# Attention and expert kernel: second-pass score units issued in pairs, and both layer norms applied by GpSimd

## The reference

```python
def _layernorm(x, eps=1e-05):
    return (x - mean(x)) / sqrt(var(x) + eps)

def attn(x, W_qkv, b_qkv, W_proj, b_proj):
    qkv = x @ W_qkv.T + b_qkv                       # 3 x 16 heads x 8
    logits = einsum('bthc,bshc->bhts', q, k) * scale
    attn = softmax(where(causal, logits, -inf))
    return einsum('bhts,bshc->bthc', attn, v) @ W_proj.T + b_proj

def ffn(x, Wg, alpha, ln_w, ln_b, fc1_w, fc1_b, fc2_w, fc2_b):
    top_vals, top_idx = top_k(x @ Wg, 2)
    comb = (one_hot(top_idx) * softmax(top_vals)).sum() * alpha
    for e in range(8):
        a = gelu(layernorm(x, ln_w[e], ln_b[e]) @ fc1_w[e] + fc1_b[e])
        out += (a @ fc2_w[e] + fc2_b[e]) * comb[:, e]

x = x + attn(_layernorm(x), ...)
x = x + ffn(_layernorm(x), ...)
```

## Time and profile before

| | |
|---|---|
| median of 3 runs | 556.99 us (554.35 to 557.75) |
| the profiled execution | 553.86 us |
| its span, first to last instruction | 551.8 us |
| mean granted TensorE clock | 0.964 of full |
| busy: TensorE, weight loads | 484.6, 306.0 us |
| busy: VectorE, ScalarE, GpSimd | 350.7, 319.7, 256.5 us |
| span by stage | attention to about 382 us, experts to 528 us, sums and output to 552 us |

### The profile page before, as it was taken

One profiled execution on the slowest core, in us unless ns is written; L12 is line 12 of the kernel. 1 busy time (PEld: TensorE's weight loads), 2 busy tenths in 40 slices (PEclk: granted clock), 3 DMA queues, 4 the chain that ended last, 5 costly groups with the idle time before them and its releaser, 6 DMA issues.

```text
span 551.8 us, 13646 instructions
## 1 busy us (share of the span) xinstructions
PE 484.6 (88%) x4736; PEld 306.0 (55%) x4736; DVE 350.7 (64%) x900; ACT 319.7 (58%) x693; POOL 256.5 (46%) x371
## 2 busy tenths in 40 slices
PE   3278999999899999999999999888999999999920
PEld 1134445445455545545544555444888888888920
DVE  3386857778868968977877887864355722222326
ACT  2126677667667656667666766666555546465610
POOL 5755132243644445454454362352766774445520
PEclk9679999999999999999999999998999999999985
DMA  2514124133225134233314230226884697666539
GB/s 67 131 35 118 43 83 116 64 92 111 94 64 148 54 85 137 72 94 113 96 63 118 72 97 27 77 70 198 248 303 154 212 317 206 212 191 194 157 138 325
DMA packets 54068, 71.67 MB, mean 130 GB/s; under 512 B 11889, under 2 KB 39704, under 8 KB 54000
## 3 DMA queue, kind: packets, MB, share of 16 engines
q1 hardware_dynamic: 48336, 59.48, 36.4%
q0 software_dynamic: 4512, 8.70, 4.8%
q10 hardware_dynamic: 1152, 2.62, 1.4%
HBM read 36.49 MB, written 20.94 MB: 104 GB/s over the span
## 4 chain that ended last, share of the span: by engine, by line
PE 64%; DVE 24%; DMA 4%; issue 3%; POOL 2%; ACT 1%; SPq 1%; POOLq 0%; DVEq 0%; ACTq 0%
DVE row_max L976 11%; PE scores L783 11%; PE acc_bank L720 11%; PE acc_bank L792 10%; PE banks L702 7%; PE banks L706 6%; PE scores L682 4%; PE scores L687 4%; PE banks L651 3%; DMA y_in<-y_dram 2%; PE banks L638 2%; DVE xn L931 2%; PE banks L735 2%; PE banks L800 1%; PE banks L747 1%
## 5 line engine op out<-in xcount | busy, mean ns | idle before, releaser
L976 DVE TENSOR_REDUCE row_max<-scores 128x2 f32<-128x1024 f32 (+2 forms) x192 | 197.3, 1041 | 67.4 <-PE scores L687 63.0
L849 ACT ACTIVATE probs<-banks 128x512 f32<-128x512 f32 (+2 forms) x384 | 183.1, 531 | 89.9 <-PE banks L706 89.3
L706 PE MATMUL banks<-stack_q,stack_k 64*128 64x256 bf16 (+3 forms) x512 | 107.3, 296 | 0.0
L702 PE MATMUL banks<-causal_back,select 64*128 64x128 bf16 (+1 forms) x768 | 100.4, 237 | 5.6 <-DVE max_rows L982 3.1
L879 ACT ACTIVATE hidden<-scores,w_in 128x256 f32<-128x256 f32 (+1 forms) x156 | 62.9, 455 | 61.2 <-PE scores L783 61.0
L720 PE MATMUL acc_bank<-probs,v 128*32 128x512 f32 (+3 forms) x1024 | 95.3, 445 | 0.5 <-issue 0.4
L1321 POOL DMA_INDIRECT y_dram<-y,z_in x71 | 69.7, 982 | 53.0 <-DVE y L1160 36.2
L1282 POOL DMA_INDIRECT z_dram<-z,pos x64 | 62.9, 983 | 45.4 <-DVE pos L1068 27.3
L682 PE MATMUL scores<-causal,select 64*128 64x128 bf16 (+1 forms) x768 | 70.4, 241 | 14.6 <-DMA stack_k<-parts 8.2
L687 PE MATMUL scores<-stack_k,stack_q 64*128 64x256 bf16 (+3 forms) x512 | 75.4, 302 | 0.0
L702 PEld LDWEIGHTS banks<-causal_back,select 64*128 64x128 bf16 x768 | 49.1, 94 | 45.3 <-ACT probs L849 18.9
(11 more groups left out here) (172 smaller groups left out, 508.2 us busy)
## 6 DMA issues: line engine op xcount, KB each, us to landing
w_in<-in_wpack SPq DMA_DIRECT2D x39, 516.0 KB, 3.9
o_dram<-oT SPq DMA_DIRECT2D x32, 256.0 KB, 2.4
stack_k<-parts SPq DMA_DIRECT2D x47, 128.0 KB, 2.4
stack_q<-parts SPq DMA_DIRECT2D x45, 128.0 KB
z_in<-z_dram SPq DMA_DIRECT2D x32, 132.0 KB, 3.8
xt<-in_x SPq DMA_DIRECT2D x8, 256.0 KB, 3.4
onT<-o_dram SPq DMA_DIRECT2D x8, 256.0 KB, 3.4
o_inv<-inv_dram SPq DMA_DIRECT2D x8, 256.0 KB, 3.5
```

The lines of the kernel that those rows point to most:

```text
L702: pe.matmul(cols[:, :, 0:P], select[rows(t), step, :], causal_back[rows(t), step, 0:len(heads), :], start=step == 0, stop=False, skip_grou ...
L706: mm = pe.matmul(cols[:, i, :], k[rows(t), at_head, blk * P:blk * P + P], q[rows(t), at_head, blk * P:T], start=False, stop=True, skip_gro ...
L849: act.activation(probs_of(n), columns(n), ACT.Exp, scale=SCALE).then_inc(s_exp, 1)
L976: dve.tensor_reduce(largest, used, AX.X, ALU.max).then_inc(s_max, 1)
```

## The change

It has three parts. First, `pass2` is issued for two units at once: it waits for both banks, writes the masks of both alternately, then the scores of both alternately, and raises `s_pass2` once for the pair. The pair stands at odd ticks, `LAG` goes from 26 to 27, and with it the product with v moves to even ticks and the copy of the output by one tick. Second, `xn` and `z` are computed by GpSimd instead of VectorE, in four tensor_scalars each, at the same places of the schedule; z still waits for the earlier dispatches from its buffer. Third, the second norm gets its own `mean_var_two`, and VectorE waits before it overwrites the moments until GpSimd has used them.

```diff
-LAG = 26
+LAG = 27
...
-        if 0 <= n - LAG < G * UNITS:
-            add(("pass2", n - LAG))
+        if 0 <= n - LAG < G * UNITS and (n - LAG) % HALVES == 0:
+            add(*(("pass2", n - LAG + t) for t in range(HALVES)))
...
             def pass2(n):
-                g, u, w, heads = unit_of(n)
+                if n % HALVES > 0:
+                    return
+                g, u, w, _ = unit_of(n)
                 b, hg = divmod(g, NG)
-                wait_bank(pe, ("pass2", n))
+                for t in range(HALVES):
+                    wait_bank(pe, ("pass2", n + t))
                 if u == 0:
                     pe.wait_ge(s_mrow[g % 2], 16 * (g // 2 + 1))
-                cols = columns(n)
+                cols = [columns(n + t) for t in range(HALVES)]
+                heads = [UNIT[u + t][1] for t in range(HALVES)]
                 blk = NT - w // P
                 q, k = stack[0][b % STACKS], stack[1][b % STACKS]
-                t = place(g, heads[0])[0]
                 for step in range(2):
-                    pe.matmul(cols[:, :, 0:P], select[rows(t), step, :], causal_back[rows(t), step, 0:len(heads), :],
-                              start=step == 0, stop=False, skip_group_check=True)
-                for i, h in enumerate(heads):
-                    at_head = place(g, h)[1]
-                    mm = pe.matmul(cols[:, i, :], k[rows(t), at_head, blk * P:blk * P + P], q[rows(t), at_head, blk * P:T],
-                                   start=False, stop=True, skip_group_check=True)
+                    for t in range(HALVES):
+                        pe.matmul(cols[t][:, :, 0:P], select[rows(t), step, :], causal_back[rows(t), step, 0:len(heads[t]), :],
+                                  start=step == 0, stop=False, skip_group_check=True)
+                for i in range(len(heads[0])):
+                    for t in range(HALVES):
+                        at_head = place(g, heads[t][i])[1]
+                        mm = pe.matmul(cols[t][:, i, :], k[rows(t), at_head, blk * P:blk * P + P], q[rows(t), at_head, blk * P:T],
+                                       start=False, stop=True, skip_group_check=True)
                 mm.then_inc(s_pass2, 1)
...
             def pass2(n):
                 g, u, w, _ = unit_of(n)
-                wait(act, s_pass2, n + 1)
+                wait(act, s_pass2, n // HALVES + 1)
...
             def aggregate(*_):
-                mean_variance()
+                wait(dve, s_xn, variance_no[0])
+                mean_variance(mean_var)
...
-            def make_z(b):
+            def find_ratio(b):
                 wait(dve, s_rtwo, b + 1)
-                wait(dve, s_disp[b % 2], 16 * 2 * NT * (b // 2))
-                normalise(z[:, b % 2, 0, :, 0:C], xt[:, NT * b:NT * b + NT, :], rstd_two[:, 0, :]).then_inc(s_z, 1)
                 dve.tensor_tensor(ratio[:, :], var_two[:, 0, :], rstd_two[:, 0, :], ALU.mult).then_inc(s_ratio, 1)
...
+            def normalise(dst, src, moments, by):
+                return pool.tensor_scalar(dst, src, moments[:, 0:1], by, ALU.subtract, ALU.mult)
+
+            def ln_apply(b, n):
+                if n == 0 and b > 0:
+                    wait_filled(pool, ("xnT", b - 1))
+                wait(pool, s_rstd, b + 1)
+                ins = normalise(xn[:, n, :], xt[:, NT * b + n, :], mean_var[:, n, :], rstd[:, n:n + 1])
+                if n == NT - 1:
+                    ins.then_inc(s_xn, 1)
+
+            def make_z(b):
+                wait(pool, s_rtwo, b + 1)
+                wait(pool, s_disp[b % 2], 16 * 2 * NT * (b // 2))
+                for n in range(NT):
+                    last = normalise(z[:, b % 2, 0, n, 0:C], xt[:, NT * b + n, :], mean_var_two[:, n, :], rstd_two[:, 0, n:n + 1])
+                last.then_inc(s_z, 1)
```

More of the change, by code:

```diff
@@ L279, in build @@
         mean_var = sb("mean_var", [P, NT, 2])
+        mean_var_two = sb("mean_var_two", [P, NT, 2])
         var_eps = sb("var_eps", [P, NT])
@@ L530, in stack_up @@
                 else:
-                    sp.wait_ge(s_pass2, (b - STACKS + 1) * NG * UNITS)
+                    sp.wait_ge(s_pass2, (b - STACKS + 1) * NG * UNITS // HALVES)
                 if b >= STACKS and i == 0 and part == 0:
@@ L602, in load_tile @@
                     sp.wait_ge(s_pass1, G * SCORED)
-                    sp.wait_ge(s_pass2, (B - 1) * NG * UNITS)
+                    sp.wait_ge(s_pass2, (B - 1) * NG * UNITS // HALVES)
                 sp.wait_ge(s_table, list_of(i) + 1)
@@ L910, in variance, with mean_variance @@
                 stats_no[0] += 1
-            def mean_variance():
+            def mean_variance(dst):
                 dve.wait_ge(s_stats, stats_no[0])
                 for n in range(NT):
-                    last = dve.bn_aggr(mean_var[:, n, :], stats[:, n, :])
+                    last = dve.bn_aggr(dst[:, n, :], stats[:, n, :])
                 link(last)
             def aggregate(*_):
-                mean_variance()
+                wait(dve, s_xn, variance_no[0])
+                mean_variance(mean_var)
                 dve.tensor_scalar(var_eps[:, :], mean_var[:, :, 1], EPS, None, ALU.add).then_inc(s_var, 1)
@@ L923, in aggregate_two @@
             def aggregate_two(b):
[L925 to L931, removed]
-                                             ALU.subtract, ALU.mult)
-                return last
+                wait(dve, s_z, b)
+                mean_variance(mean_var_two)
+                dve.tensor_scalar(var_two[:, 0, :], mean_var_two[:, :, 1], 1.0 + EPS, EPS * EPS, ALU.mult, ALU.add)
+                dve.tensor_scalar(var_two[:, 1, :], mean_var_two[:, :, 1], EPS, None, ALU.add).then_inc(s_two, 1)
             def init_stacks():
@@ L940, in ln_stats @@
                 variance(xt[:, NT * b:NT * b + NT, :])
-            def ln_apply(b, n):
-                if n == 0 and b > 0:
-                    wait_filled(dve, ("xnT", b - 1))
-                wait(dve, s_rstd, variance_no[0])
-                ins = normalise(xn, xt[:, NT * b:NT * b + NT, :], rstd, (n,))
-                if n == NT - 1:
-                    ins.then_inc(s_xn, 1)
             def split(b, i, step):
@@ L1052, in combine @@
                 link(dve.tensor_reduce(alpha_of[:, :, :].rearrange("p j n -> p (j n)"), by_alpha[:, :, :], AX.X, ALU.add))
+                wait(dve, s_disp[b % 2], 16 * 2 * NT * (b // 2))
                 dve.tensor_copy(z[:, b % 2, :, :, ID].bitcast(I32), token_ids[:, :, NT * b:NT * b + NT])
@@ L1327, in _ @@
             walk({"init_masks": init_masks, "init_stacks": init_stacks, "init_second": init_second, "init_third": init_third, "init_v": init_v, "init_experts": init_experts,
-                  "init_blank": init_blank, "init_wide": init_wide, "dispatch": dispatch, "turn_y": turn_y, "ln_agg": rsqrt, "r_root": rsqrt_two, "split": split, "max_parts": split_max,
+                  "init_blank": init_blank, "init_wide": init_wide, "dispatch": dispatch, "turn_y": turn_y, "ln_agg": rsqrt, "ln_apply": ln_apply, "r_root": rsqrt_two, "r_z": make_z, "split": split, "max_parts": split_max,
                   "residual": residual, "r_exp": second_gate})
```

4 lines of the change are left out of this document (2 added, 2 removed).

## The result

The changed kernel takes 602.72 us (median of 4 runs, 601.86 to 606.04) against 555.76 us (554.35 to 557.75) for the kernel before on the same chip: ratio 1.087, 95% interval 1.084 to 1.090. That is 47 us slower, 27 us above the upper end of the forecast range.

A forecast was written before the change was run, and what follows sets the result against it. TensorE, busy 484.6 of 551.8 us, was taken as the bound. Savings and waits net -0.4 us a batch, -2.8 over seven; with +2.6, +0.4 and +1.4 that is +1.6: 555.5, or 558 us on the median's footing, range 540 to 576.

The forecast's parts named there:

- The savings: Pass 2 on TensorE: in 17 of 24 pairs a batch the second unit's own time goes, 6.4 us a batch.
- (a) to (d): Waits added in attention because a pair needs both banks free and written: 1.7, 1.8, 1.0 and 0.6 us a batch.
- the credit: 0.5 us a batch off the added waits, since VectorE's max_rows already held pair 3's second unit in some groups.
- (a): Two-block to one-block pair, once a group: waiting for ScalarE cancels the four one-block savings, 1.7 us a batch.
- (b): Pair 2 waits for both banks of pair 1, the maximum's transpose holding the third: 0.45 us a group, 1.8 a batch.
- (e): xn on GpSimd behind a dispatch DMA: its transpose 1.0 us later, 0.4 of savings lost, 1.4 us a batch.
- (f): z in a steady batch on GpSimd: ready about 0.5 us ahead of its transpose, so no cost.
- (g): z of the last batch, in the expert stage, queued behind a scatter on GpSimd: 2.6 us later, once.
- (h): GpSimd's queue at the start: xn of batch 0 0.3 us later, of batch 1 0.4 earlier, counted as nothing.
- (i): LAG 27 at the end: one more pass 2 step without pass 1, 0.4 us, and bare bank waits, 1.4 us.
- Slow GpSimd: Rival: GpSimd's tensor_scalar takes 0.9 us, making xn and z late, 4 us a batch, 586 us; chance 0.12.
- the clock: Rival: longer idle at xn's transposes and late z lowers TensorE's granted clock, 14 us in all, 572 us; chance 0.17.

The follow-up runs named there:

- e17: Kernel before with only pass 2 in pairs and LAG 27, norms on VectorE, on a chip where before takes 554 us: ratio 1.0067.
- e1: Kernel before with only pass 2 in pairs and LAG 27, norms on VectorE, first measurement, on a slower chip: ratio 0.9999.
- e13: Kernel before with only pass 2 in pairs and LAG 27, norms on VectorE, repeated on a slower chip: ratio 0.997.
- e8: Changed kernel with xn normalised for only 40 of 128 columns, the others left zero: ratio 1.044 to the kernel before.
- e15: Changed kernel with the four xn operations put ahead of the dispatch's DMA on GpSimd's queue: ratio 1.047 to the kernel before.
- e7: Kernel before with only z moved to GpSimd, no pairing: 612 to 632 us against 591, too scattered for a ratio.
- e4: Kernel before with only pass 2 in pairs, at LAG 26, norms on VectorE, on a slower chip: ratio 0.987.
- e9: Kernel before with only pass 2 in pairs, at LAG 26, norms on VectorE: 544.6 us against 554.3, ratio 0.981.
- e12: The kernel before, unchanged, run once more for its profile: 555.49 us.

## Why the prediction was wrong, by its steps

The mechanism of each step was found where the prediction put it; the price of one operation, the pairs' savings and the clock's toll were mis-sized, and a joint case was missing. The steady batch was forecast at 43.7 us (44.1 - 0.4) and measured 50.8. Between them lie 1.5 us of the pairing's, 1.7 of the longer gap at xn, 1.5 of the wait for z and 2.8 of the clock, less the 0.4 that the forecast had put beside the gap at xn; all but the first follow from the price of the operation.

**Pairing.** The savings (6.4 us a batch) measured 4.7, the mis-sized term. My reading, not measured apart: the single units that I counted at their full 0.43 or 0.37 us lay partly beside pass 1 already; I took this off for two units, and it holds for more. The waits (a) to (d), with the credit, came to 4.6 and measured 4.4; one by one, (a) is 0.46 at 258.52 and (b) 0.45 at 263.12, as forecast. Net -0.3 in place of -1.8 us a batch, some 11 us over seven. In one batch each of e17, e1 and e13 the clock fell behind the usual wait for max_rows as well; in e17 that batch took 45.4 us instead of 43.9. The rule cited ahead of the result (the Trainium skill, TensorEngine Tiling (Array Packing), PSUM Bottleneck) put the pairing nearer to nothing, and e17's 1.0067 agrees with it.

**(e) xn, the step that failed.** I took 0.33 us for GpSimd's tensor_scalar between bounds of 0.29 and 1.15; it is 0.79. The lower bound was a plain copy; this operation also applies two values per partition, and its price lies near the middle. Each engine's operations on xn, before on VectorE and after on GpSimd (count, then ns at least, median and at most):

```profile
L931 DVE TENSOR_SCALAR xn<-xt,mean_var,rstd x32: 334/340/514, 6.3 to 281.7; 128x128 f32<-128x128 f32 x32
```
```profile
L1224 POOL TENSOR_SCALAR xn<-xt,mean_var,rstd x32: 785/790/804, 6.4 to 317.9; 128x128 f32<-128x128 f32 x32
```

So GpSimd needs 2.3 times VectorE's 0.34 us. (z's median on VectorE is 0.338 us too; the 488 ns of the earlier trace rows are a mean that a few long ones raise.) All 32 on GpSimd lie within 19 ns, whatever ran beside them, so contention did not make the price. The Trainium skill, GPSIMD Engine Reference, Engine selection, calls one-input work roughly line-rate; this trace does not agree, the ratio is nearer to the two times that it gives for two inputs. Four operations cost 1.8 us more than my sum, and the gap is 3.8 us, not 2.2.

**(f) z.** "0.5 us ahead" plus 1.8 us is 1.3 late; measured 1.49. The rival named 0.45 us as the price from which z comes late; 0.79 is well past it.

**(g) z in the expert stage.** 2.6 forecast, 4.04 measured: the same 1.8 us, less a little. **(h)** the start: nothing forecast; TensorE waits 2.1 us longer for xn of batch 0 and 1.7 us for batch 1. **(i)** LAG 27 at the end: 1.8 us forecast; in e17 the lag behind the kernel before grows from 1.7 us at the z transpose that ends the steady batches (302.82 against 301.07) to 4.3 at the last one (410.45 against 406.16), so about 2.5.

**The rivals.** "Slow GpSimd" at 0.9 us gave 586 and "the clock" gave 572, with 0.12 and 0.17. Both happened, and the first causes the second: a slower xn is what opens the gap behind which the clock falls. I had priced them as exclusive. Added, 586 - 558 and 572 - 558 give 600, beside the measured 602.7; in part by luck, since a fall of the clock costs 2.8 us and not the 1.7 I took from the earlier trace rows, but comes in fewer places than the eight I counted. So beside the size of (e) the error was to leave the joint case out: its time lay beyond the range.

## What to carry to other kernels

An operation that no row shows has its price between its bounds until something measures it; if a short step later decides on it (here 0.45 us), the forecast is the two cases with their chances, not the lower bound. Rivals that share a cause are one case: here a late operand on TensorE's path cost its wait (3.8 us) and, where the clock fell behind it, 2.8 us more. Issuing two units in one go paid here only where the banks behind it came free in time: moving it by one tick was worth 0.013 to 0.026, more than the idea as first placed.

## What the runs showed of the hardware

GpSimd's tensor_scalar with two per-partition operands took 0.79 us for 128 columns and 0.50 for 40: an estimate from these two widths is 0.36 us fixed and 3.3 ns a column. The granted clock fell to 0.50 behind the steady gaps of 3.4 to 3.9 us, behind most of 2.4 (e8, e15) and some of about 2 (e7: three of five), and, with the pairing, behind one of 1.09 (e17, 283.44: 0.50 from 284 to 286). It stayed at 1.00 behind one of 2.76 (changed kernel, 118.67) and, in the kernel before, behind each 1.17 us of the steady batches. The length of one gap does not decide alone.

On the slower chips the batches until about 300 us are only a little longer. The same kernel (e4 there, e9 here) starts a z transpose at 298.31 against 293.59 us, its last one at 424.44 against 397.41, and ends at 585.0 against 543.1: most of the time is lost late. The chain of e1, on such a chip, has pieces that no work of this core explains (start us, us, what):

```profile
371.53 5.55 another core or an unknown queue
```

One more, at 451.23, is 14.7 us long; e4 has one of 13.2 us at 442.77. The chains of the kernel before, the changed kernel, e9, e12 and e17, on the other chips, have none. What holds the engines up there stays open.
